# The first residual of a four-layer model assembled on chip instead of through a DRAM scratch, with its norm in three groups

## What is computed

```
h = patches(x) @ W.T + b                        # 8 images x 64 patches, 768 -> 192
h = concat([h, text_rows], axis=1)              # 8 x (64 + 77) rows of 192
h = h + mamba_block(layernorm(h), ...)          # the block starts with a layernorm of its own
h = h + quantized_ffn(layernorm(h), ...)
h = h + attention(layernorm(h), ...)
h = h + mixture_of_experts(layernorm(h), ...)
```

## Time and profile before

| what | value |
|---|---|
| median of 3 runs | 764.42 us (764.05 to 764.9) |
| the profiled execution's own time | 764.11 us |
| its span | 762.3 us |
| mean granted TensorE clock, share of full | 0.912 |
| busy: PE, DVE, ACT, POOL | 84%, 64%, 49%, 37% of the span |

### The profile page before, as it was taken

How to read it: one execution, slowest core, us unless ns; L and a number is a source line. 1 busy time by engine, 2 the same in 40 slices (tenths; PEclk the granted TensorE clock), 3 DMA queues, 4 the chain that set the end, 5 groups by cost and what they waited for, 6 DMA issues and landing times.

```text
span 762.3 us, 13399 instructions
## 1 busy us (share of the span) xinstructions
PE 642.0 (84%) x4916; PEld 575.3 (75%) x4916; DVE 485.5 (64%) x1254; ACT 371.9 (49%) x857; POOL 279.3 (37%) x293
## 2 busy tenths in 40 slices
PE   2329899898989936739899999799989999999994
PEld 2328776578989722328788888698989999999993
DVE  3368779562250788674877774388358777777752
ACT  0027876771342538456566543341136565565551
POOL 2534515344020335013432434101313675675633
PEclk9759999996999956659999999789979999999998
DMA  7810000215000091300000002103155677688843
GB/s 220 192 45 5 2 1 1 94 39 148 1 1 1 4 253 29 114 0 5 3 5 4 3 6 84 45 1 115 37 223 172 179 241 244 188 240 229 190 130 67
DMA packets 30412, 67.89 MB, mean 89 GB/s; under 512 B 6890, under 2 KB 20755, under 8 KB 28011
## 3 DMA queue, kind: packets, MB, share of 16 engines
q0 software_dynamic: 13200, 48.20, 21.8%
q1 hardware_dynamic: 17147, 18.84, 9.1%
HBM read 60.90 MB, written 6.61 MB: 89 GB/s over the span
## 4 chain that ended last, share of the span: by engine, by line
PE 46%; DVE 6%; ACT 2%; issue 2%; POOL 1%; another core or an unknown queue 1%; POOLq 0%; DVEq 0%; ACTq 0%
PE bank L1856 10%; PE bank L1816 4%; PE bank L1820 4%; PE bank L1819 4%; PE bank L1818 4%; PE bank L1817 4%; PE bank L1736 2%; PE bank L1672 2%; PE bank L1715 2%; DVE amx L2423 1%; PE bank L1692 1%; PE bank L1722 1%; PE bank L1634 1%; PE bank L1698 1%; DVE big L2429 1%
## 5 line engine op out<-in xcount | busy, mean ns | idle before, releaser
L2498 DVE TENSOR_SCALAR big<-bank 128x256 f32<-128x256 f32 (+1 forms) x126 | 52.1, 414 | 60.5 <-PE bank L1820 55.1
L1271 ACT ACTIVATE big<-bank 128x256 f32<-128x256 f32 (+1 forms) x126 | 47.6, 379 | 57.5 <-PE bank L1820 53.8
L797 POOL TENSOR_TENSOR big<-big,arc 128x423 f32<-128x423 f32 (+1 forms) x48 | 37.8, 814 | 77.5 <-DVE arc L2443 77.5
L824 POOL DMA_INDIRECT total<-big,goal x32 | 53.6, 1675 | 24.0 <-issue 17.3
L1816 PE MATMUL bank<-x_lead,w_lead 128*128 128x256 f32 x192 | 56.4, 294 | 0.0
L1819 PE MATMUL bank<-x_both,w_lead 128*128 128x256 f32 x192 | 54.5, 284 | 0.0
L1820 PE MATMUL bank<-x_both,w_rest 128*128 128x256 f32 x192 | 54.1, 282 | 0.0
L1818 PE MATMUL bank<-x_lead,w_rest 128*128 128x256 f32 x192 | 54.0, 281 | 0.0
L1817 PE MATMUL bank<-x_rest,w_lead 128*128 128x256 f32 x192 | 53.8, 280 | 0.0
L831 POOL DMA_INDIRECT big<-x_rows,origin x32 | 33.4, 1042 | 48.9 <-DVE goal L2555 23.2
L2509 DVE SCALAR_TENSOR_TENSOR big<-big 128x256 f32<-128x256 f32 (+1 forms) x126 | 50.3, 410 | 0.0
(11 more groups left out here) (532 smaller groups left out, 2010.2 us busy)
## 6 DMA issues: line engine op xcount, KB each, us to landing
big<-in_patches SPq DMA_DIRECT2D x1, 1536.0 KB, 7.6
areg<-in_e_gate_up SPq DMA_DIRECT2D x1, 1536.0 KB, 6.6
shared_lead<-in_e_gate_up POOLq DMA_DIRECT2D x1, 1536.0 KB, 7.0
wreg<-in_ffn_w SPq DMA_DIRECT2D x1, 1152.0 KB
ffw_lead<-in_ffn_w POOLq DMA_DIRECT2D x1, 1152.0 KB, 7.1
out<-total SPq DMA_DIRECT2D x2, 423.0 KB
wreg<-in_in_w SPq DMA_DIRECT2D x2, 419.0 KB
wreg<-in_in_w SPq DMA_DIRECT2D x4, 209.5 KB
```

What stands on the lines that cost most here:

```text
L824: pool.indirect_dma_start(out=total, in_=YS[:, j % 2, q * D:(q + 1) * D], in_offset=None, out_offset=bass.IndirectOffsetOnAxis(ap=goal[:, ...
L1271: nc.scalar.activation(GS[:, n % 3, 0:w], bank[2 * (n % 2)][:, 0:w], ACT.Silu).then_inc(S["g_silu"], 1)
L2498: v.tensor_scalar(UM[:, n % 3, 0:w], bank[2 * (n % 2) + 1][:, 0:w], 10.0, -10.0, ALU.min, ALU.max).then_inc(S["u_clip"], 1)
```

## The change

The DRAM scratch `h0` and its eleven transfers are gone; `H` is made on chip, three tiles at a time.

- Ids are found in the row layout of `H`. `score` and `following` (the token after) are zeroed tiles of 76 x 1152, filled at the columns of text rows. PE transposes both by tile (9 + 9), ACT copies the second from PSUM (`follow`), DVE picks nine times. `shf` and `nxt` give way to one tile `win`, loaded by ACT's queue, which now also loads `tokw`, `tokb` and `ln1`. The patches come in two halves.
- POOL gathers nine times 128 rows (`words`); the rows of images get row 0 of the table, which `known` masks.
- POOL makes three matrices of shifted identities (`shift`, `shift_even`, `shift_odd`, 128 x 384). PE multiplies each pair of images by slices of them (`place`, 11 matmuls), which moves the rows to their place in the tile's PSUM bank and gives zero elsewhere. DVE adds the masked words into `H` (`together`).
- The norm runs per group of three tiles. DVE's masks now stand ahead of the images.
- The six POOL loads of fp32r weights are four ACT copies, and POOL's four subtractions are DVE's (`weight_rests`).
- ACT, not DVE, makes the fp32 value under the rest (`XS1`, now two buffers). The third group is transposed after project(0).
- The weight loads of the second layer share one semaphore (`ld_q`) where they had three.

The core of the diff:

```diff
-            load(shf, window(76, 0, NX), "ld_tok")
-            load(nxt, window(NX, 1, 76), "ld_tok")
-            load(patches, i["patches"].rearrange("(k p) n -> p k n", p=P), "ld_embed")
+            for u in range(2):
+                part = slice(u * 2 * P, (u + 1) * 2 * P)
+                load(patches[:, :, part], i["patches"][:, part].rearrange("(k p) n -> p k n", p=P), ("ld_img0", "ld_img1")[u])
...
-            sp.wait_ge(S["img_ready"], 2)
-            for b in range(NB):
-                sp.dma_start(h0[b, 0:NI, :], img[(b % 2) * NI:(b % 2 + 1) * NI, b // 2, :]).then_inc(S["h_loaded"], 16)
-            sp.wait_ge(S["txt_ready"], 3)
-            sp.dma_start(h0[:, NI:L, :].rearrange("b n d -> n b d"), txt).then_inc(S["h_loaded"], 16)
-            sp.wait_ge(S["h_loaded"], 16 * (NB + 1))
...
+            st.add(pool.memset(shift, 0.0))
+            st.add(pool.memset(score, 0.0))
+            st.add(pool.memset(following, 0.0))
...
+            for t in range(TT):
+                pool.indirect_dma_start(out=words[:, t, :], out_offset=None, in_=i["emb"],
+                                        in_offset=bass.IndirectOffsetOnAxis(ap=ids[:, t:t + 1], axis=0))\
+                    .then_inc(gathered[t // 3], 16)
...
+            for d in range(2):
+                cols = slice(d * DCOLS, d * DCOLS + WCOLS)
+                nc.scalar.copy(INH[:, cols], in_full[:, cols]).then_inc(S["in_lead"], 1)
+                nc.scalar.copy(INBH[:, cols], in_both[:, cols]).then_inc(S["in_lead"], 1)
+            deviations(0, ln_var, 3, ln_std)
+            second_deviations(0)
+            deviations(1, ln_var, 6, ln_std)
+            second_deviations(1)
+            deviations(2, ln_var, 9, ln_std)
+            first_tokens(0)
+            second_deviations(2)
+            first_tokens(1)
+            first_tokens(2)
...
+            def place(j):
+
+                pe.wait_ge(S["img_ready"], j + 1)
+                for b in (2 * j, 2 * j + 1):
+                    for t, a, z in IMG_ROWS[b]:
+                        s_, at = (shift_odd, P + NI) if b % 2 else (shift_even, P)
+                        at -= b * L - t * P
...
+                        last = mm(bank[k][:, o:o + D], s_[:, at:at + P], img[:, j, :], start=b == owners[0], stop=b == owners[-1])
...
+            for j in range(3):
+                image(j)
+            together(0)
+            image(3)
+            first_inverse(0)
+            weight_rests(0)
+            together(1)
+            twice_normal(0)
+            first_inverse(1)
+            together(2)
+            twice_normal(1)
+            first_inverse(2)
+            first_rests(0)
+            twice_normal(2)
+            weight_rests(1)
+            first_rests(1)
+            first_rests(2)
```

More of the change, by code:

```diff
@@ L645, in _ @@
[L645 to L655 removed]
+            st.wait()
@@ L1305, in _ @@
             pe.wait_ge(S["const_ready"], 9)
-            pe.wait_ge(S["p_step"], 2)
-            pe.wait_ge(S["txt_ready"], 1)
-            for b in range(NB):
-                last = nc.tensor.transpose(bank[2 + b // 4][0:NX, (b % 4) * 76:(b % 4 + 1) * 76], score[:, b * NX:(b + 1) * NX],
-                                           identw[0:76, 0:76])
-                if b % 4 == 3:
-                    last.then_inc(S["scoreT"], 1)
-            pe.wait_ge(S["ld_embed"], 48)
+            pe.wait_ge(S["p_step"], 9)
@@ new lines, in _ @@
+            for a, z in FOLLOW:
+                for t in range(a, z):
+                    last = nc.tensor.transpose(bank[6 + a // 6][:, (t - a) * 76:(t - a + 1) * 76], following[:, t * P:(t + 1) * P], identw[0:76, 0:76])
+            last.then_inc(S["scoreT"], 1)
+            pe.wait_ge(S["txt_ready"], 1)
+            for a, z in FOLLOW:
+                for t in range(a, z):
+                    last = nc.tensor.transpose(bank[2 + a // 6][:, (t - a) * 76:(t - a + 1) * 76], score[:, t * P:(t + 1) * P], identw[0:76, 0:76])
+                last.then_inc(S["scoreT"], 1)
@@ new lines, in place @@
+            def place(j):
[4 more added lines that the diff above has]
+                        at -= b * L - t * P
+                        owners = [c for c in range(NB) for u, _a, _z in IMG_ROWS[c] if u == t]
+                        k, o = IMG_AT[t]
+                        last = mm(bank[k][:, o:o + D], s_[:, at:at + P], img[:, j, :], start=b == owners[0], stop=b == owners[-1])
+                last.then_inc(S["img_mm"], 1)
@@ new lines, in _ @@
+            v.tensor_scalar(score[:, 0:T].rearrange("p (b n) -> p b n", n=L)[:, :, NI:L], run.rearrange("p (b n) -> p b n", n=NX),
+                            128.0, qcol[0:76, :], ALU.mult, ALU.add).then_inc(S["txt_ready"], 1)
+            for u, (a, z) in enumerate(FOLLOW):
+                dve.wait_ge(S["scoreT"], u + 2)
+                st.add(v.tensor_reduce(best[:, a:z], bank[2 + u][:, 0:(z - a) * 76].rearrange("p (a b) -> p a b", b=76), AX.X, ALU.max))
+            st.wait()
+            dve.wait_ge(S["next_out"], 2)
@@ new lines, in together @@
+            def together(g):
+                dve.wait_ge(gathered[g], 48)
+                dve.wait_ge(S["img_mm"], IMG_PLACED[g + 1])
+                if g == 2:
+                    dve.wait_ge(S["padded"], 1)
+                for t in range(3 * g, 3 * (g + 1)):
+                    k, at = IMG_AT[t]
+                    r = rows(t)
+                    st.add(v.scalar_tensor_tensor(out=H[0:r, t, :], in0=words[0:r, t, :], scalar=known[0:r, t:t + 1], in1=bank[k][0:r, at:at + D],
+                                                  op0=ALU.mult, op1=ALU.add))
+                st.wait()
+                for t in range(3 * g, 3 * (g + 1)):
+                    st.add(v.bn_stats(stats[:, t, :], H[:, t, :]))
+                st.wait()
+                for t in range(3 * g, 3 * (g + 1)):
+                    v.bn_aggr(mv[:, t, :], stats[:, t, :]).then_inc(ln_var, 1)
```

263 lines of the change are left out of this document (138 added, 125 removed).

## The result

| | before | changed |
|---|---|---|
| median of the runs | 764.66 us (764.05 to 766.46, 4 runs) | 756.96 us (755.86 to 757.96, 4 runs) |
| the profiled execution's own time | 764.11 us | 757.55 us |
| its span | 762.3 us | 755.7 us |
| mean granted clock | 0.912 | 0.919 |

A forecast was written before the change was run, and what follows sets the result against it. The head, not an engine, was taken to set the time, waiting for H through the scratch. 15.0 gained at the third projection, minus 1.0 clock and 0.7 hand-overs, gave 13.3 us: 751.1, own range 748.5 to 754, 8 in 10 747.5 to 756.

The forecast's parts named there:

- Term 1: Finding the ids at the start: no gain, ids out at 15.6 us as before, bounds 14.5 and 17.
- Term 2: Embedding, image placing and gathers: first group's H can be made at 23.0 us, gathers costing nothing while PE is later.
- Term 3: DVE's norm chain from the first H to all rests: 20.15 us plus 1.2 of waits, ending at 44.35.
- the mark: Start of the third projection, project(2), at 59.35 us before; its shift shortens the program equally, gain there 15.0 us.
- Term 4: Weights' landing and ACT's copies: first copy at 19.9 us, no cost; 1.4 us lost if landing stays at 22.8.
- Term 5: PE's clock starting low at the projections: 1.0 us lost, bounds 0 and 2.
- Term 6: Hand-overs between engines: some fourteen blocks waiting on semaphores at 0.05 us each, 0.7 us lost.
- late gathers: Rival at the head: first words land late, at 25.3 us, delaying DVE; time 753.5 to 756, chance 12%.

The follow-up runs named there:

- e5: Changed kernel with patches and embedding weights asked for only when both token loads have landed; 0.9877 of the kernel before.
- e9: Changed kernel with tokens loaded first, tokb on its own semaphore, masks early, and idle matmuls at the head and in three later pauses; 0.9891 of the kernel before.
- a0: Changed kernel without further edit, timed again in the following job, on chip 9; 0.9872 of the kernel before.
- a2: Changed kernel without further edit, timed again in a later job, on chip 0; 0.9859 of the kernel before.
- f1: Changed kernel with tokb on its own semaphore, masks early, and image rows asking for 128 different table rows; 0.9899 of the kernel before.
- f0: Changed kernel with tokb on its own semaphore and the masks ahead of DVE's wait for tokens; 0.9893 of the kernel before.
- f2: Changed kernel with tokb apart, masks early, and in_w onward asked for only after the first three gathers land; 766.92 us, one run, beside 766.63 before.
- g1: Changed kernel with tokb apart, masks early, only the second direction's in_w behind the first three gathers, its ACT copies later; 0.9866 of the kernel before.
- e1: Changed kernel with tokb on a semaphore of its own, so PE does not wait for it; 0.9895 of the kernel before.
- e3: Changed kernel with the nine gathers replaced by memsets of the words; 0.9874 of the kernel before.
- a1: Changed kernel without further edit, timed a third time as the mark of its job; 0.9893 of the kernel before.
- e8: Changed kernel with 34 idle matmuls at the head and 17 more in three later PE pauses; 0.9889 of the kernel before, median 756.67 us.
- f3: Changed kernel with tokb apart, masks early, image rows asking for different table rows, and 51 idle matmuls; 0.9863 of the kernel before.
- e4: Changed kernel with the four 838-column subtractions moved back from DVE to POOL; 0.995 of the kernel before.

## Why the prediction was wrong

The sign was right, and so was the main mechanism: the wait for the scratch went, and by the four ratios 8 to 11 us arrive at the end. The size was off by 5.6 us in the medians. By the prediction's own steps:

- **Term 1, ids at 15.6: wrong, 18.07.** I took the tokens at 7.3 because their issue is shorter. But the patches (SP, 1.23) and `tokw` (ACT's queue, 1.40) are asked for right behind, and the tokens' short rows share the engines with them; e5, where they are alone, has DVE start at 7.58 and ids at 15.06, inside my bounds. A smaller part: DVE's first comparison took 1.28 us where it took 0.80 before, beside POOL's cast of the same length of row, which the change put there (0.80 again in e9, where the cast is over by then). I applied the rule that asking earlier helps only as far as the engines were idle to `in_w`, and not to the tokens.
- **Term 2, first `H` at 23.0: wrong, 30.14, and 27.1 to 27.3 in a0 and a2.** This is the step that failed. It failed twice over. Two microseconds from the end of POOL's instruction to the landing came from the last gather of the kernel before, 3.0 from its start, at a DMA share of 0.36 (25 to 28 us); here the first three meet `in_w`, and take 5.8 to 6.2 from the start of the third (f1, f0, a0), 4.9 to 5.2 from its end. f2 and g1 give 3.1 from the start without it. And PE's start, put at 12.7, was 16.82. The patches are not the reason, though their halves take 12.8 us in the median to land where the whole took 7.6: by the trace's semaphore events the first half is there at 11.90. PE waits for `tokw` and `tokb`; e1, where they are told apart, starts at 15.26 with `tokw`, which takes 13.8 us to land:

```profile
big<-in_tok_w ACTq DMA_DIRECT2D x1, 576.0 KB, 13.8
```

PE alone would have held the first `H` until 26.74 (e3). The masks, which I put on the path, were not on it.
- **Between 27.3 and 30.1** lie 2.8 us that the first profile and a1 have and a0 and a2 have not. They are PE's and not the gathers': in the first profile the semaphore of the first three gathers is complete at 27.25, and PE's own reaches the count that `together` waits for at 30.05, though the record of the placing matmul that raises it ends at 27.05. In a0 this event (26.52) and the record's end (26.51) agree. DVE sits idle 3.75 us ahead of the third image in the first profile, 5.31 in a1 and 4.35 in e8; f0 has such a lag at the fourth image. e9, f1 and f3, on the chip of a1, do not show it, nor does any profile from chips 9 and 0. Why PE signals so long after its records stays open.
- **Term 3, DVE's chain: right.** From the first `together` to the mark 50.78 - 30.14 = 20.6 us, with DVE busy 19.1 of them; I had 21.35.
- **Term 4, the weights: wrong landing, right cost.** The first copy started at 24.57, not at 19.9, and no earlier than before (22.81). The Trainium skill's rule in "DMA: Bandwidth & Descriptors", section "Issuing engines are not separate DMA queues", which I named against me, describes what happened. The late landing cost nothing, as the first deviation was wanted only at 32.5.
- **Term 5, clock -1.0: right in the first profile (8.6 at the mark, 7.5 at 64), 2.2 in a0.** **Term 6** can't be told apart from term 3.
- **"What the change moves the mark by, the program is shorter by": wrong.** I found nothing behind the mark that waits for the head; but the clock's falls do not stay where they were. Of the gain at the mark, 1.7 to 9.0 us are gone at 484 in the table's profiles (e1, whose profiled run was its slowest, is the 9.0), and none in e8. The first profile's 8.6 us become 5.5 there and 6.6 in the span. Some 2.6 to 2.9 us of the loss are in every profile of the changed kernel: the fall at 203, and the stay at 1.2 GHz about 300 that is 10.3 us long and not 6.9. The rest (the falls at 50, 86 and 118 to 130) comes and goes. That e8 keeps its gain speaks for the clock as the cause; its profile is a single one, and no ratio tells it from the changed kernel.
- **One reading** was loose, with nothing resting on it: the clock's first fall shows in the second slice already (7) and lasts from 30.4 to 57.7 us in the trace; the third slice is only the lowest.

So of the 6.4 us missed at the mark, 7.1 are the first `H` and -0.7 the chain. Of the 7.1, 2.8 are PE's late signal, whose cause is open. The other 4.3 follow from a0: its third gather was through POOL at 22.1 where I had 19.9 (2.2, the ids' part), it took 5.2 us more to the first `H` where I had 2.0 (3.2, the traffic), less 1.1 of slack that I had left between the words at 21.9 and `H` at 23.0. By PE's path alone it would have been 3.7 (e3). I gave late gathers 12% and 753.5 to 756, for the wrong reasons (POOL held by DVE, or one hot row).

## What to carry to other kernels

When a change starts transfers earlier, list what else is asked for in the same microseconds: a landing time read from a quiet stretch does not hold in a busy one (3.1 us against 6 here), and a semaphore shared by several loads makes each reader wait for the last. When several waits end within a microsecond, removing one shows nothing; take them out together before calling any of them free. And in a kernel whose PE clock falls in its pauses, a gain at the head arrives at the end with a few microseconds of play (the same kernel kept 5.8 of 11.3 us once and 9.1 of 11.6 another time): profile the same kernel twice before reading a few microseconds out of one.

## What the hardware showed that I had not expected

- A DVE instruction of 3 columns held for 7.26 us through four POOL instructions without getting in between (e4); a comparison of 616 columns stretched from 0.80 to 1.28 us beside one POOL cast of 0.70.
- The same kernel, with heads equal to 0.3 us, has spans 3.7 us apart through falls of the clock in other places (a0 and a2, on two chips that run the kernel before in the same time; a0's own five runs lie 3.4 us apart on one chip), and idle matmuls that keep the clock in one pause can be followed by 14 us at 1.2 GHz in a stretch that had none (f3).
- In the changed kernel's embedding the first 24 records took 6.98 us from 16.82 on and the next 12 took 2.11 (timeline below), at a granted clock of 1.00 throughout: 0.29 us a record at first and 0.18 later, which the granted clock does not show. No run here isolates the reason.

```profile
16.82 6.98 PE L1359 MATMUL bank<-big 128*128 128x192 f32 x24 [1.45 <-DMA big<-in_tok_b]
24.28 2.11 PE L1359 MATMUL bank<-big 128*128 128x192 f32 x12
```
